# A Taylor-feature attention and a six-layer local-attention transformer in one kernel: first transfers, block sums, Wo's product and the order list changed

## Chip, cores and metric

The kernel runs on one core of one Trainium2 chip. The metric is the device time of one launch in microseconds (us). A profiled execution gives the trace; other executions give the times.

## What is computed

Input x is 8 sequences of 512 tokens with 128 features, all float32. With `ln` a normalisation over the features without weights:

```
y = x + ln(first(ln(x)))           # first: linear attention with Taylor features
out = y + ln(stack(ln(y)))         # stack: six layers

first: q, k = h Wq', h Wk'  (16 heads of 16);  v = h Wv'  (16 heads of 64)
       f(z) = [1, z/2, (z x z)/(4 sqrt 2)];  A = tril(f(q) f(k)')
       y = A v; y = y * rsqrt(mean(y^2) + 1e-5) * g;  return y Wo'
stack, six times:
       q, k, v = split(x Wqkv); q, k = scaled unit vectors, rotary tables
       local attention over windows of 32 (own window and the one before)
       x = x + attention Wo
       x = x + (a * gelu(gate)) W2 + b2,  a, gate = split(norm(x) W1 + b1)
```

Both halves work on tokens shifted by one in half of the features. f(q)f(k)' is (1 + s/4)^2/2 + 1/2 up to a common factor, s being the product of q and k: so the kernel forms the squares, adds 1 and masks only in the 128x128 blocks on the diagonal. For the blocks left of it the "+1" is a constant times the sum of v over earlier blocks of 128 tokens. These are the block sums of the title: sums of h over the first 128, 256 and 384 tokens (`CS`, four columns, the first zero), times Wv.

## The kernel before, in words

One Python function, `order` (with the class `Order`), writes a list of stages. Every stage has a place on a time axis (`PLACE`), the list is sorted by place, and each of the five engine programs walks the list and emits its share of every stage. So the places set the order of instructions on each engine and nothing else; waits on semaphores do the rest. Each engine works in its own order and never overtakes. `group` and `put(..., banks=...)` give each stage that writes PSUM the next bank of a ring (two banks in the first attention, three in the stack) and record which stage must have freed it.

**The start.** `sync_program` issues all first transfers on SP's queue: the constants C (2756 columns), VEC, two staged constants, Wq and Wk and Wv of the first attention, its Wo, and then x of the first sequence (stage AL). GpSimd (POOL) copies Wq and Wk three times into a wider layout in AO (L1250), ScalarE (ACT) rounds all weights to float32r in WH, six pieces (L1001), and VectorE (DVE) takes the rest, WL = w - WH (L783), after it has cast the staged constants. Only then do ACT and DVE start on the list.

**The first attention** has 24 slots for each of 8 sequences (b): AL transposes x, N1 to N4 normalise it (N4 spreads the factor, AX multiplies it in, on DVE, and forms `CS` by three reductions, L806), AC multiplies the block sums by Wv (16 float32 products of 128x128 weights by 4 columns), ACd copies them to cumt. AQ and AV are the projections, each three float32r products (high by high, high by low, low by high), AS the scores, ASa the square (ACT), ASd the mask (DVE), AY scores by v, AE adds the block sums to AY's result. AR, AI, AM and AO finish: root mean square and Wo. All of it is software-pipelined over b by the places.

**The stack** has units u = 8 layer + b, each of 8 slots n (384 slots in all) and 4 pairs m of slots. PJ projects q and k of two heads (2 per slot), PQ squares (ACT, L1177), PT multiplies by the rotary tables (DVE, L891), TS swaps rows by DMA (SP, L445), AD adds the swapped rows (POOL, L1312), SS sums squares, NM1 and NM2 make the norms, RW and RB write them out and spread them over 64 partitions by DMA (SP, L453 and L463), PR multiplies k by them (POOL, L1294). S1 (PE) needs both PR of its pair; then MX (DVE, L915, L920), S3 (exponentials, ACT, L1201), SU (DVE, L926), NP (POOL, L1317), TT (DVE, two transposes, L936 and L937), PX (SP, DMA PP<-PX, L470), PV (PE, four parts), PVn (ACT copy to AOT, L1214). Once per unit: WO (eight float32 products AOT by LO on PE in one piece, 16 records in the trace; two adds on DVE), F1 to F3 (normalisation; F2n on DVE is L956 to L960, F3 spreads on PE, H on DVE, XCH on ACT, XCL by POOL in F3l), F4g and F4a (three pairs of products, GELU and gate), F5. XS and XSl round the next unit's input.

Every product on PE stands at L480 in the trace, since all go through the helper `mm`; float32 products leave two records each, float32r ones a single record. A row names the moving operand first and the weights second: PS<-LXH,LH is PJ's first product, PS<-LH,LXH is VP's (the v projection), PS<-CS,WH is AC's.

Of the kernel before, what the change touches and what calls it, by code (L numbers as in the profile page):

```python
# [6 lines left out]
F32 = mybir.dt.float32  # L7
# [8 lines left out]
F1 = 341  # L16
# [20 lines left out]
    "AVa": -0.03, "AS": -1.00, "ASa": -0.95, "ASd": -0.82, "AY": 0.90, "AE": 2.85, "AEa": 3.56,  # L37
    "AR": (14.32, 25.00), "AI": (25.06, 26.09, 27.44), "AM": (28.75, 0.64), "AMd": 0.10, "AO": (30.62, 0.53),
    "NM": (35.69, 37.69, 37.84, 40.22), "AZ": 39.99, "NX": (44.40, 45.04, 45.20, 47.87), "AW": 47.72,
}  # L40

CONST = {}
# [93 lines left out]
def order():  # L136
# [94 lines left out]
    for u in range(NB * DEPTH):  # L231
# [6 lines left out]
        at(z + P["WO"], group, "WO", u, "wo_dve", 2 * u + 2)  # L238
# [44 lines left out]
def build(nc, xin, cst, awq, awk, awv, awo, wqkv, wo, w1, w2, vec, out):  # L283
    o = order()
    no = o.no
    with ExitStack() as ctx:
# [13 lines left out]
        with ExitStack() as ca:  # L300
# [7 lines left out]
            CS = [sb(f"CS{i}", [128, 4], F32, ca) for i in range(2)]  # L308
            XR = [sb(f"XR{i}", [128, L], F32, ca) for i in range(4)]
# [97 lines left out]
        def sync_program(e):  # L407
            on = Waits(e)
            e.dma_start(C[:, :], cst[:, 0:KEPT]).then_inc(sem["c_in"], 16)
            e.dma_start(VEC[:, :, :], vec).then_inc(sem["vec_in"], 16)  # L410
            n_sel = CONST_COLS - KEPT
            e.dma_start(Vf[:, 0:n_sel], cst[:, KEPT:CONST_COLS]).then_inc(sem["sel_in"], 16)
            e.dma_start(Vf[:, 3072:3328], awq).then_inc(sem["awq_in"], 16)
# [3 lines left out]
            for st, key in o.line:  # L417
                if st == "AL":
                    b, = key
                    if b:  # L420
                        on.wait_ge("al_pe", b)
# [55 lines left out]
        def tensor_program(e):  # L477
# [14 lines left out]
            for st, key in o.line:  # L492
# [208 lines left out]
                elif st == "WO":  # L701
# [5 lines left out]
                    for hp in range(8):  # L707
                        p = mm(bk(st, key)[:, :], LO[:, hp, :], AOT[:, hp, :], hp == 0, hp == 7)
# [674 lines left out]
```

## Time and profile before

| | |
|---|---|
| median of three runs | 3833.57 us (3826.7 to 3837.46) |
| profiled execution | 3838.31 us, span of its records 3836.5 us |
| PE busy | 3549.6 us (93%) |
| DVE, ACT, POOL busy | 2627.8, 2549.0, 2022.4 us (68, 66, 53%) |
| chain that ended last | PE 69%, DVE 12%, ACT 7%, issue 5%, DMA 3%, SPq 2%, POOL 1% |
| first transfers | C 1378 KB, two staged constants 768 KB, Wv and Wo 512 KB each, x 256 KB, Wq and Wk 128 KB each |

A span is cut into stretches by time from its first record. Busy is the time in which an engine had an instruction in work; PE's is modelled from pipelined products, so the start-to-start distance of its rows says more than their durations. PEclk is the granted clock of TensorE as a share of 2.4 GHz: 0.50 is 1.2 GHz. "[0.88 <-X]" after a row is time in which the engine sat idle before it, and what ended that. The chain is followed back from the last instruction, each step to what released it.

### The profile page before, as it was taken

How to read it: one execution, taken by the hardware profiler on the slowest of the kernel's cores; microseconds unless marked ns; L12 is line 12 of the kernel's file. 1: busy time of each engine (PE TensorE's matmuls, PEld its weight loads, DVE VectorE, ACT ScalarE, POOL GpSimd, SP SyncE). 2: the span in 40 equal slices, each digit the busy share in tenths (PEclk: the TensorE clock that was granted, in tenths of full speed). 3: DMA queues.
4: the chain of work that ended last, by engine and by line, in shares of the span. 5: the costliest groups of instructions: out<-in, count | busy, mean ns of one | idle time of the engine just before them, and what ended most of it. 6: DMA issues, size and time to landing. Idle time of an engine off the chain costs nothing.

```text
span 3836.5 us, 149435 instructions
## 1 busy us (share of the span) xinstructions
PE 3549.6 (93%) x65224; PEld 2293.5 (60%) x65416; DVE 2627.8 (68%) x3583; ACT 2549.0 (66%) x5965; POOL 2022.4 (53%) x1564
## 2 busy tenths in 40 slices
PE   7999998799999999999999999999999999999997
PEld 4555554466666666666666666666666666666664
DVE  3555555577777777777776777777777777767662
ACT  4655564476767676777666766777767767677773
POOL 0000000666666666666666666666666666666651
PEclk9999999799999999999999999999999999999997
DMA  1000000333333333333333433333433333433330
GB/s 49 6 6 6 6 6 3 130 129 117 123 125 132 121 124 121 122 130 129 118 121 114 138 123 123 115 124 121 136 117 128 113 132 120 134 113 126 126 109 25
DMA packets 222618, 389.72 MB, mean 102 GB/s; under 512 B 63758, under 2 KB 101900, under 8 KB 221836
## 3 DMA queue, kind: packets, MB, share of 16 engines
q1 hardware_dynamic: 196080, 364.42, 27.5%
q10 hardware_dynamic: 25884, 15.73, 1.4%
q8 instruction: 514, 8.42, 0.9%
q14 instruction: 140, 1.15, 0.1%
HBM read 124.14 MB, written 7.34 MB: 34 GB/s over the span
## 4 chain that ended last, share of the span: by engine, by line
PE 69%; DVE 12%; ACT 7%; issue 5%; DMA 3%; SPq 2%; POOL 1%; ACTq 0%; POOLq 0%; DVEq 0%
PE PS L480 68%; ACT SC L1201 4%; DVE MX L915 2%; DMA RB<-root_scratch 2%; DVE TPB L891 2%; DVE SM L926 2%; DVE PX L937 1%; DMA PP<-PX 1%; POOL K L1294 1%; DVE VAR L958 1%; ACT AOT L1214 1%; DVE H L965 1%; ACT XCH L1072 1%; DVE VAR L956 1%; DVE BQ L920 1%
## 5 line engine op out<-in xcount | busy, mean ns | idle before, releaser
L891 DVE SCALAR_TENSOR_TENSOR TPB<-PS,VEC,C 128x1024 f32<-128x1024 f32 x768 | 961.0, 1263 | 98.4 <-ACT SX L1177 89.2
L1201 ACT ACTIVATE SC<-PS,BQ,RQ 128x64 f32<-128x64 f32 x3072 | 966.2, 430 | 26.0 <-DVE BQ L920 25.6
L1294 POOL TENSOR_TENSOR K<-K,RB 128x512 f32<-128x512 f32 x384 | 492.4, 1282 | 727.2 <-DMA RB<-root_scratch 726.7
L480 PEld LDWEIGHTS PS<-PP,VV 32*64 32x64 f32 x24576 | 436.1, 133 | 314.0 <-issue 210.8
L480 PE MATMUL PS<-PP,VV 32*64 32x64 f32 (+1 forms) x24576 | 542.0, 223 | 72.1 <-ACT AOT L1214 32.9
L1177 ACT ACTIVATE SX<-PS 128x512 f32<-128x512 f32 x768 | 475.5, 628 | 195.0 <-PE PS L480 188.8
L926 DVE TENSOR_REDUCE SM<-SC 128x16 f32<-128x1024 f32 x192 | 234.2, 1220 | 388.7 <-ACT SC L1201 388.6
L1312 POOL TENSOR_TENSOR K<-TPB,TR 128x512 f32<-128x512 f32 x384 | 493.8, 1286 | 0.0
L1312 POOL TENSOR_TENSOR Q<-TPB,TR 128x512 f32<-128x512 f32 x384 | 492.9, 1284 | 0.0
L1317 POOL TENSOR_TENSOR SC<-SC,RC 128x1024 f32<-128x1024 f32 x192 | 366.2, 1907 | 158.1 <-DVE RC L928 154.5
L480 PE MATMUL PS<-LXH,LH 128*128 128x512 f32 x768 | 350.2, 456 | 16.9 <-DVE TPB L891 9.8
L1191 ACT COPY VV<-PS 128x512 f32<-128x512 f32 x384 | 238.3, 620 | 188.6 <-PE PS L480 185.5
L1214 ACT COPY AOT<-PS 128x1024 f32<-128x1024 f32 x192 | 197.3, 1028 | 248.0 <-PE PS L480 246.1
L480 PE MATMUL PS<-AOT,LO 128*128 128x512 f32 x768 | 338.6, 594 | 0.0
L480 PEld LDWEIGHTS PS<-K,Q 64*32 64x32 f32 x24576 | 255.8, 105 | 126.2 <-issue 80.5
L480 PE MATMUL PS<-K,Q 64*32 64x64 f32 (+1 forms) x24576 | 294.1, 225 | 35.0 <-issue 19.4
L480 PE MATMUL PS<-LXH,LL 128*128 128x512 f32 x768 | 305.4, 398 | 0.0
L480 PE MATMUL PS<-LXL,LH 128*128 128x512 f32 x768 | 304.9, 397 | 0.0
L1260 POOL TENSOR_TENSOR XR<-XR,T 128x512 f32<-128x512 f32 x8 | 12.9, 1611 | 524.0 <-DVE T L862 524.0
L480 PE MATMUL PS<-SX,C 128*32 128x128 f32 x6144 | 253.3, 281 | 4.8 <-ACT SX L1177 3.0
L1133 ACT ACTIVATE PA<-PS 128x768 f32<-128x768 f32 (+1 forms) x192 | 169.8, 884 | 128.2 <-PE PS L480 127.1
L915 DVE TENSOR_REDUCE MX<-PS 128x16 f32<-128x1024 f32 x192 | 234.0, 1219 | 25.4 <-PE PS L480 24.7
(166 smaller groups left out, 6076.8 us busy)
## 6 DMA issues: line engine op xcount, KB each, us to landing
TR<-TPB SPq DMA_DIRECT2D x768, 256.0 KB, 2.7
RB<-root_scratch SPq DMA_DIRECT2D x768, 128.0 KB
PP<-PX SPq DMA_DIRECT2D x192, 192.0 KB, 2.6
WS<-in_wqkv ACTq DMA_DIRECT2D x72, 128.0 KB, 2.5
PP<-PX SPq DMA_DIRECT2D x192, 48.0 KB, 2.3
root_scratch<-NV SPq DMA_DIRECT2D x384, 8.0 KB
LO<-in_wo ACTq DMA_DIRECT2D x6, 512.0 KB, 4.6
T<-in_x SPq DMA_DIRECT2D x8, 256.0 KB, 3.0
```

The lines of the kernel that those rows point to most:

```text
L480: return e.matmul(dst, lhsT, rhs, start=start, stop=stop, **kw)
L891: e.scalar_tensor_tensor(TPB[:, n % 3:4 + n % 2:3 + n % 2 - n % 3, w, :], g, VEC[:, l, 9 + w:10 + w], C[:, at:at + 1024].rearrange("p (o c ...
L915: e.tensor_reduce(MX[:, :], g, AX_X, ALU.max).then_inc(sem["s1_dve"], 1)
L926: e.tensor_reduce(SM[:, :], SC[m % 2][:, :, :, :].rearrange("p g x k -> p g (x k)"), AX_X, ALU.add).then_inc(sem["su_dve"], 1)
L1133: e.activation(P[t % 3][:, :, 0:n], PS[:, 2 * (t % 2):2 * (t % 2) + 2, 0:n], ACT.Square, bias=1.0, scale=0.25).then_inc(sem["as_act"], 1)
L1177: e.activation(SX[i % 3][:, :], bk("PJ", key)[:, :], ACT.Square).then_inc(sem["pj_act"], 1)
L1191: e.copy(VV[:, c, 512 * hf:512 * hf + 512], bk("VP", key)[:, :]).then_inc(sem["vp_act"], 1)
L1201: p = e.activation(SC[m % 2][:, g, :, :].rearrange("p x k -> p (x k)"), bank[s][:, at:at + 64], ACT.Exp, bias=BQ[m % 2][:, g:g + 1], scale ...
L1214: e.copy(AOT[:, 2 * p % 8:2 * p % 8 + 2, :], PS[:, 2:4, :]).then_inc(sem["pv_act"], 1)
L1294: e.tensor_tensor(dst, dst, RB[n % 2][:, :], ALU.mult).then_inc(sem["pr_pool"], 1)
L1312: e.tensor_tensor((Q, K)[w][:, n % 8, :], TPB[:, n % 3, w, :], TR[n % 2][:, w, :], ALU.add).then_inc(sem["ad_pool"], 1)
L1317: e.tensor_tensor(sc, sc, RC[m % 2][:, :].rearrange("p (g o) -> p g o", o=1).broadcast_to([128, 16, 64]), ALU.mult).then_inc(sem["np_pool" ...
```

## The change

C is loaded in two transfers: columns 0 to 707 first, the rotary tables (2048 columns) last with a semaphore of their own (`tab_in`), for which the first PT waits. x of sequence 0 is SP's second transfer. Wq, Wk and Wv of the first attention are issued on ACT's queue, ahead of its table load. DVE splits `CS` into a float32r high part and the rest (`CX`, eight columns, two more small instructions for each b), and AC takes 16 float32r products, of 8 and of 4 columns, in place of 16 float32 ones; ACd adds the two halves by a reduction. WO's product becomes a stage WO (the first two of eight products) and three stages WOp (two each), each with its own wait for PVn; the adds on DVE follow the last. All places are new.

Sorted, the new places change the order of the stack as follows. The unit that the rows show is that of slots 192 to 199 (pairs m = 96 to 99, PJ 400 to 415), in the trace from 1985 to 2048 us.

- PE: the third part of PV stands ahead of the two SS of its slot, was behind. WO(23) stood between PJ(409) and the fourth part of PV(96); its pieces now stand ahead of PJ(409): WO, PV(96, 2), SS, SS, WOp, WOp, WOp, PJ(409). F3 stood ahead of PJ(413), now behind.
- Banks: VP, PJ, WO, F1 to F5 and RQ take three banks in turn. PJ(410) took its bank from PJ(409) and takes it from WO; F1 took it from WO and takes it from PJ(409); PJ(414) took it from F3 and takes it from PJ(413), which is free once PT(413) has run on DVE.
- DVE: TT stands ahead of NM1, was behind; WO's adds stand ahead of PT(409), were behind.
- POOL: the two AD of a slot stand ahead of its PR, were behind; XSl stands behind the next PR, was ahead.
- ACT: XS stands ahead of VC. SP: the order is the same.

In the first attention AS stands some 0.4 slots earlier, AE 0.3 earlier, AV ahead of N1 for the first sequences; AC stays behind AR and between two AS.

```diff
@@ -26,17 +26,18 @@
 PLACE = {
-    "S1": 0.07, "MX": 0.18, "S3": (0.52, 0.62, 1.38, 1.44), "SU": 1.45, "NP": 1.74, "TT": 2.63, "PX": 2.78,
-    "PV": (3.60, 3.67, 4.87, 5.14), "PVn": 5.23, "PJ": (-7.60, -7.06), "PQ": (-7.54, -7.13),
-    "PT": (-7.37, -6.95), "TS": -6.56, "SS": -6.40, "AD": -5.68, "NM1": -3.39, "NM2": -2.98, "RW": -2.86,
-    "RQ": -1.78, "RB": -2.15, "PR": -1.83, "XS": -9.54, "XSl": -9.24, "VP": -0.60, "VC": -0.55, "WO": 13.08,
-    "F1": 13.91, "F2": 14.08, "F2n": 14.42, "F3": 14.93, "F3l": 14.71, "TB": (15.66, 15.92),
-    "F4": (15.76, 15.79, 15.83), "F5": 17.32, "E1": 18.17, "EN": (18.53, 19.02, 19.08, 19.73), "E2": 19.50,
-    "E3": 20.36, "AL": -35.20, "NI": (-33.38, -31.57, -31.13, -29.38), "AX": -29.38, "AXp": -29.48,
-    "AC": -22.55, "ACd": -22.70, "AQ": (-8.65, -8.07), "AQa": 0.01, "AQd": 0.03, "AV": (-9.18, 2.33),
-    "AVa": -0.03, "AS": -1.00, "ASa": -0.95, "ASd": -0.82, "AY": 0.90, "AE": 2.85, "AEa": 3.56,
-    "AR": (14.32, 25.00), "AI": (25.06, 26.09, 27.44), "AM": (28.75, 0.64), "AMd": 0.10, "AO": (30.62, 0.53),
-    "NM": (35.69, 37.69, 37.84, 40.22), "AZ": 39.99, "NX": (44.40, 45.04, 45.20, 47.87), "AW": 47.72,
+    "S1": 0.070, "MX": 0.204, "S3": (0.520, 0.817, 1.345, 1.440), "SU": 1.481, "NP": 2.090, "TT": 2.494,
+    "PX": 2.428, "PV": (3.608, 3.721, 4.542, 5.121), "PVn": 5.291, "PJ": (-7.527, -7.038),
+    "PQ": (-7.490, -7.100), "PT": (-7.376, -6.920), "TS": -6.667, "SS": -6.381, "AD": -5.837, "NM1": -3.382,
+    "NM2": -3.273, "RW": -2.978, "RQ": -1.794, "RB": -2.203, "PR": -1.824, "XS": -9.729, "XSl": -8.095,
+    "VP": -0.654, "VC": -0.535, "WO": (12.494, 12.664, 12.743, 12.755), "F1": 13.903, "F2": 14.160,
+    "F2n": 14.420, "F3": 15.011, "F3l": 15.140, "TB": (15.648, 16.315), "F4": (15.746, 15.781, 15.832),
+    "F5": 17.288, "E1": 17.542, "EN": (18.253, 18.621, 18.733, 19.195), "E2": 19.234, "E3": 20.274,
+    "AL": -33.742, "NI": (-32.832, -32.109, -30.652, -29.154), "AX": -29.060, "AXp": -26.947, "AC": -22.855,
+    "ACd": -22.643, "AQ": (-8.619, -8.246), "AQa": -0.094, "AQd": -0.306, "AV": (-9.421, 2.424), "AVa": -0.196,
+    "AS": -1.374, "ASa": -1.037, "ASd": -0.890, "AY": 0.975, "AE": 2.559, "AEa": 3.552, "AR": (15.747, 25.047),
+    "AI": (25.064, 25.483, 27.445), "AM": (28.750, 0.727), "AMd": -0.720, "AO": (30.708, 0.580),
+    "NM": (35.565, 37.690, 38.161, 40.725), "AZ": 40.998, "NX": (44.350, 45.008, 45.145, 46.999), "AW": 46.923,
 }
@@ -235,7 +236,9 @@
             at(z + j + P["VC"], o.put, "VC", 8 * u + j)
-        at(z + P["WO"], group, "WO", u, "wo_dve", 2 * u + 2)
+        at(z + P["WO"][0], group, "WO", u, "wo_dve", 2 * u + 2)
+        for i in range(1, 4):
+            at(z + P["WO"][i], o.put, "WOp", u, i)
         at(z + P["F1"], group, "F1", u, "f1_act", 2 * u + 2)
@@ -306,6 +309,7 @@
             CS = [sb(f"CS{i}", [128, 4], F32, ca) for i in range(2)]
+            CX = [sb(f"CX{i}", [128, 8], F32R, ca) for i in range(2)]
             XR = [sb(f"XR{i}", [128, L], F32, ca) for i in range(4)]
@@ -406,19 +410,19 @@
             on = Waits(e)
-            e.dma_start(C[:, :], cst[:, 0:KEPT]).then_inc(sem["c_in"], 16)
-            e.dma_start(VEC[:, :, :], vec).then_inc(sem["vec_in"], 16)
+            tab = CONST["tab"][0]
+            e.dma_start(C[:, 0:tab], cst[:, 0:tab]).then_inc(sem["c_in"], 16)
+            e.dma_start(T[2][:, :].rearrange("p (a d) -> p a d", a=4),
+                        xin[0].rearrange("(a p) d -> p a d", p=128)).then_inc(sem["x_in"], 16)
             n_sel = CONST_COLS - KEPT
             e.dma_start(Vf[:, 0:n_sel], cst[:, KEPT:CONST_COLS]).then_inc(sem["sel_in"], 16)
-            e.dma_start(Vf[:, 3072:3328], awq).then_inc(sem["awq_in"], 16)
-            e.dma_start(Vf[:, 3328:3584], awk).then_inc(sem["awk_in"], 16)
-            e.dma_start(AOf[:, 2048:3072], awv).then_inc(sem["awv_in"], 16)
             e.dma_start(WOA[:, :, :], awo.rearrange("p (c d) -> p c d", c=8)).then_inc(sem["awo_in"], 16)
+            e.dma_start(VEC[:, :, :], vec).then_inc(sem["vec_in"], 16)
+            e.dma_start(C[:, tab:KEPT], cst[:, tab:KEPT]).then_inc(sem["tab_in"], 16)
             for st, key in o.line:
-                if st == "AL":
-                    b, = key
-                    if b:
-                        on.wait_ge("al_pe", b)
+                if st == "AL" and key[0]:
+                    b, = key
+                    on.wait_ge("al_pe", b)
                     e.dma_start(T[2][:, :].rearrange("p (a d) -> p a d", a=4),
@@ -546,16 +550,15 @@
                     b, = key
-                    on.wait_ge("cs_dve", 3 * b + 3)
+                    on.wait_ge("cs_dve", 5 * b + 5)
                     on.wait_ge("aw_act", 6)
                     on.wait_ge("aw_dve", 6)
-                    on.wait_ge("zero_pool", 2)
                     free(on, st, key)
...
                         c = slice(2048 + 128 * hp, 2176 + 128 * hp)
-                        mm(g[:, 4 * hp:4 * hp + 4], WH[:, c].bitcast(F32), CS[b % 2][:, :], hp == 0, False, skip_group_check=True)
-                        p = mm(g[:, 4 * hp:4 * hp + 4], WL[:, c].bitcast(F32), CS[b % 2][:, :], False, hp == 7, skip_group_check=True)
+                        mm(g[:, 8 * hp:8 * hp + 8], WH[:, c], CX[b % 2][:, :], hp == 0, False, skip_group_check=True)
+                        p = mm(g[:, 8 * hp:8 * hp + 4], WL[:, c], CX[b % 2][:, 0:4], False, hp == 7, skip_group_check=True)
                     p.then_inc(sem["ac_pe"], 1)
@@ -703,10 +706,16 @@
                     free(on, st, key)
-                    on.wait_ge("pv_act", 4 * u + 4)
-                    for hp in range(8):
-                        p = mm(bk(st, key)[:, :], LO[:, hp, :], AOT[:, hp, :], hp == 0, hp == 7)
-                    p.then_inc(sem["wo_pe"], 1)
+                    on.wait_ge("pv_act", 4 * u + 1)
+                    for hp in range(2):
+                        mm(bk(st, key)[:, :], LO[:, hp, :], AOT[:, hp, :], hp == 0, False)
+                elif st == "WOp":
+                    u, i = key
+                    on.wait_ge("pv_act", 4 * u + i + 1)
+                    for hp in range(2 * i, 2 * i + 2):
+                        p = mm(bk("WO", (u,))[:, :], LO[:, hp, :], AOT[:, hp, :], False, hp == 7)
+                    if i == 3:
+                        p.then_inc(sem["wo_pe"], 1)
                 elif st == "F1":
@@ -804,6 +813,12 @@
                         e.tensor_reduce(CS[b % 2][:, i:i + 1], T[3][:, 0:128 * i], AX_X, ALU.add).then_inc(sem["cs_dve"], 1)
+                    on.wait_ge("zero_pool", 2)
+                    on.wait_ge("cs_dve", 5 * b + 3)
+                    e.tensor_copy(CX[b % 2][:, 0:4], CS[b % 2][:, :]).then_inc(sem["cs_dve"], 1)
+                    on.wait_ge("cs_dve", 5 * b + 4)
+                    e.tensor_tensor(CX[b % 2][:, 4:8], CS[b % 2][:, :], CX[b % 2][:, 0:4].bitcast(F32),
+                                    ALU.subtract).then_inc(sem["cs_dve"], 1)
                 elif st == "AQd":
@@ -818,7 +833,8 @@
                         on.wait_ge("ae_dve", 8 * (b - 1))
-                    e.tensor_copy(cumt[b % 2][:, :], bk("AC", key)[:, 0:32]).then_inc(sem["ac_dve"], 1)
+                    g = bk("AC", key)[:, 0:64].rearrange("p (h x i) -> p h i x", h=8, x=2)
+                    e.tensor_reduce(cumt[b % 2][:, :].rearrange("p (h i) -> p h i", h=8), g, AX_X, ALU.add).then_inc(sem["ac_dve"], 1)
                 elif st == "ASd":
@@ -882,6 +898,7 @@
                     at = CONST["tab"][0] + 1024 * w
+                    on.wait_ge("tab_in", 16)
                     if n > 1:
@@ -935,10 +952,10 @@
                     e.transpose(PX[:, :, :], SC[m % 2][:, :, 0, :]).then_inc(sem["tt_dve"], 1)
-                elif st == "WO":
-                    u, = key
+                elif st == "WOp" and key[1] == 3:
+                    u = key[0]
                     l, b = lb(u)
-                    g = bk(st, key)
+                    g = bk("WO", (u,))
                     x0, x1 = X[0:64, b, 0:L], X[64:128, b, 1:1 + L]
@@ -990,6 +1007,9 @@
 
+            e.dma_start(Vf[:, 3072:3328], awq).then_inc(sem["awq_in"], 16)
+            e.dma_start(Vf[:, 3328:3584], awk).then_inc(sem["awk_in"], 16)
+            e.dma_start(AOf[:, 2048:3072], awv).then_inc(sem["awv_in"], 16)
             table("natural_log_exp_and_others")
@@ -1088,7 +1108,7 @@
                         on.wait_ge("ax_pool", b)
-                        on.wait_ge("cs_dve", 3 * b)
+                        on.wait_ge("cs_dve", 5 * b)
                     elif kind == "mid" and b:
```

## Rows read from the trace of the kernel before

**Rows 1.** Busy time by stretch (us): PE, weight loads, DVE, ACT, POOL; PEclk, DMA, GB/s

```profile
50.00:640.00 590.00, 584.98 (x2940) 301.51 (x2938) 325.65 (x592) 347.79 (x552) 19.32 (x13) 0.97 0.02 6
...
760.00:3740.00 2980.00, 2781.42 (x60386) 1873.69 (x60580) 2198.21 (x2829) 2104.22 (x5200) 1929.19 (x1480) 1.00 0.36 123
```

**Rows 2.** First transfers: stretch 3 to 12; Wq's to landing; chain's last step

```profile
3.00:12.00 9.00, 0.00 (x0) 0.00 (x0) 2.07 (x4) 1.15 (x3) 2.35 (x6) 1.00 0.98 386
...
VA<-in_awq SPq DMA_DIRECT2D x1, 128.0 KB, 7.3
...
4.66 8.28 DMA T<-in_x
```

**Rows 3.** Timeline, 9 to 32 us: start, duration, engine, line, operation, idle before

```profile
9.50 2.35 POOL L1250 COPY AO<-VA 128x256 f32<-128x256 f32 x6 [6.88 <-DMA VA<-in_awq]
10.85 3.22 ACT L1001 CAST WH<-AO 128x512 fp32r<-128x512 f32 x6 [8.84 <-POOL AO L1250]
11.50 3.90 DVE L783 TENSOR_TENSOR WL<-AO,WH 128x512 fp32r<-128x512 f32 x6 [0.95 <-ACT WH L1001]
14.20 0.59 ACT L1079 COPY XR<-PS 128x512 f32<-128x512 f32 x1
19.50 0.16 DVE L794 TENSOR_SCALAR N<-PS 128x4 f32<-128x4 f32 x1 [4.11 <-PE PS L480]
24.82 0.59 PE L480 MATMUL PS<-CS,WH 128*128 128x4 f32 x2 [1.96 <-DVE CS L806]
31.25 0.57 PE L480 MATMUL PS<-CS,WL 128*128 128x4 f32 x2
```

**Rows 4.** AC: busy time on PE, 40 to 600; timeline of AC(4) and AC(6)

```profile
40.00:600.00 560.00, 31.09 (x224) 0.97 0.02 6
...
276.55 0.39 PE L480 MATMUL PS<-CS,WH 128*128 128x4 f32 x2
...
280.22 1.09 PE L480 MATMUL PS<-PA,VA 128*64 128x384 f32 x4
...
434.31 0.56 PE L480 MATMUL PS<-CS,WH 128*128 128x4 f32 x2
```

**Rows 5.** PE by stretch: behind AC(1), between, behind AC(7)

```profile
52.00:64.00 12.00, 12.00 (x63) 0.72 0.00 0
64.00:116.00 52.00, 51.85 (x274) 1.00 0.02 6
...
516.00:520.00 4.00, 4.00 (x15) 0.57 0.00 0
```

**Rows 6.** Timeline of PE: short float32r products, and what follows them

```profile
102.90 0.45 PE L480 MATMUL PS<-QA,KA 64*128 64x256 f32 x4
103.28 0.87 PE L480 MATMUL PS<-PA,VA 128*64 128x384 f32 x4
```

**Rows 7.** Whom PE waited for, 760 to 3740: total us, times, longest

```profile
PE PS L480 <- DVE TPB L891: 60.1, 53, 1.2
...
PE PS L480 <- DMA PP<-PX: 26.7, 37, 1.8
PE PS L480 <- DVE VAR L960: 19.9, 44, 1.2
PE PS L480 <- POOL K L1294: 11.5, 20, 1.2
```

**Rows 8.** Timeline of the unit of slots 192 to 199, by engine

```profile
1999.84 1.66 SPq L445 DMA_DIRECT2D TR<-TPB  x2
...
2008.45 1.28 POOL L1294 TENSOR_TENSOR K<-K,RB 128x512 f32<-128x512 f32 x1 [3.64 <-DMA RB<-root_scratch]
...
2015.65 7.03 PE L480 MATMUL PS<-AOT,LO 128*128 128x512 f32 x16
...
2037.21 1.27 DVE L891 SCALAR_TENSOR_TENSOR TPB<-PS,VEC,C 128x1024 f32<-128x1024 f32 x1
...
2037.56 0.40 PE L480 MATMUL PS<-LXH,LH 128*128 128x512 f32 x1
```

## The prediction

> **What bounds the kernel now.** First the busy time by stretch [rows 1]. It shows three parts. From 50 to 640 us, in the first attention, PE is busy for 585.0 of 590 us: only PE's own work can shorten it, new places at most the 5.0 us of idle time. From 760 to 3740 us, in the stack, PE is idle for 199 us of 2980, some 4.3 us in each of 46 units, with DVE at 74% and ACT at 71%: here the order counts, and so does the question which wait ends last. Between and after them lie ramps. Second the granted clock: 0.97 in the first attention, 1.00 in the stack [rows 1]. Third the timeline of the start, where the span begins with 13 us in which PE waits for x [rows 2].
>
> **The start.** The last step of the chain is x, landed at 12.94 us behind all constants and weights [rows 2]. The DMA engines are full: 386 GB/s from 3 to 12 us at a share of 0.98. The queue carries 3730 KB up to and with x, 3.82 MB; 3.82 / 0.386 = 9.9 us, so a landing is at 3.0 us plus the megabytes ahead / 0.386. Test on Wq: 2322 KB give 9.2, measured 2.1 + 7.3 = 9.4 [rows 2]. After the change Wq and Wk (256 KB, and as much beside them on the other queue) land at 4.4, x (354 + 256 KB, as much beside) at 6.2, Wv at 7.1, the staged constants (2.20 MB) at 8.7, where they were.
> ACT converts WH before it touches the list. From POOL's start at 9.50 WH began 1.35 us later and took 3.22 [rows 3]: from 4.4 that ends at 9.0, in place of 14.1. XR moves from 14.20 to 9.0: 5.2 us. DVE begins no earlier, but it waited 0.95 us for WH [rows 3]; without this WL ends at 14.3, and DVE's next task, at 19.50 before, is due at 14.3: just covered. If not, the chain is late by what WL is late. AC(0) then starts at 24.82 - 5.2 + 0.4 (two small DVE instructions of 0.16 us and their gaps, the price of the row at 19.50 [rows 3]) = 20.0. It lasted to 31.25 + 0.43 = 31.68 [rows 3], 6.85 us for 32 records, and 16 records of the same distance take 3.4: it ends at 23.4, 8.3 us earlier. Bounds: 4 us, if the queues share otherwise and the first conversions come late, and 10 us.
>
> **AC of the other seven sequences.** AC lies in the stretch where PE has no slack, so its time counts in full. Seven AC keep PE busy for 31.09 us (224 records); AC(4), at the full clock throughout, takes 280.22 - 276.55 = 3.67 us, 0.115 for a record [rows 4]. A float32r product is one record. The trace has none of 4 or 8 columns; the nearest are four with 128 to 256 columns and 64 rows, which take 103.28 - 102.90 = 0.38 us, at most 0.095 each with its weights [rows 6]. I take the 0.115 of a float32 record, since it is as wide in weights: 7 x 16 x 0.115 = 12.8 us, gain 18.3. Bounds: a product costs as much as a whole float32 one (0.23, no gain) or nearly nothing (gain 31).
> [...]
>
> **The clock behind AC.** Behind each AC the clock falls to 0.50, 1.2 GHz: 12 us at a mean of 0.72 around AC(1) and 4 us at 0.57 behind AC(7), with 1.00 between [rows 5]. Four of the seven cost 12 x 0.28 = 3.4 us, three 4 x 0.43 = 1.7: 18.7 us in all, which is what 0.97 over 590 us says. Of this 31.09 - 7 x 3.67 = 5.4 lie inside AC and are counted above, 13.3 in the work behind it. A fall can begin early: in AC(6) the ninth of 16 pairs of records, at 434.31, is the first slow one (0.56 us), 8 x 0.23 = 1.8 us after AC's start [rows 4]. Nothing else in this part sets one off [rows 5]. An AC of 1.8 us is at the edge. I expect one of seven to remain, 1.7 us: gain 11.6. Bounds: all stay at 1.7 (gain 13.3 - 11.9 = 1.4), none (13.3).
> DVE's two added instructions and the reduction in ACd cost nothing while DVE is busy for 55%. AC's neighbours stay. The new places of AS, AE and AQ can win the 5.0 us of idle time [rows 1]; I take 2, bounds -3 and 5.
>
> **The stack.** I expect nothing, though PE waits there. The longest wait is F4's second pair for a bank: 60.1 us in 53 waits, 1.2 us at most, so nearly once in each unit, on TPB, that is PT(414) [rows 7]. PT(414) stands behind SU(99) on DVE, that behind S3(99) and XCH on ACT, that behind H, F2n and MX(99): this chain runs from S1(99)'s end, and the change moves none of its members against another. What PE gains inside it is waited out at its end. F3 behind PJ(413) removes the wait on VAR (19.9 us, 0.45 each [rows 7]): hidden.
> In return PJ(414) now waits for PT(413). That ran from 2037.21 to 2038.48 while PE began PJ(414) at 2037.56 [rows 8]: a new wait of 0.9 us, under the 1.2 us of the F4 wait. Without that cover it costs 48 x 0.9 = 43 us.
> WO is 7.03 us in 16 records [rows 8], the same in four pieces; what it passes, PJ(409), is delayed by 7 us, and behind it PQ, PT(409) and the swap by DMA for AD(408, 409). PV's last part, for which ACT waits, keeps its time, and DVE and POOL are idle during WO. PJ(410)'s bank now comes from WO's two adds, free 0.5 us before by my count of the durations.
> SS behind WO's first piece (7.03 / 4 = 1.8 us) delays NM1, which TT no longer waits for: these two about cancel, off the chain.
> POOL is the delicate place. PR(197) feeds S1(98). It waited 3.64 us for RB until 2008.45; now two AD of 1.28 us stand ahead of it. They need the swapped rows, issued from 1999.84 to 2001.5 and landed some 2.7 us later (the page's median), 4.2 us before PR: enough for 2.6 us of AD, with 1.6 to spare [rows 8]. Where the landings lie closer, PR is late by up to 2.6 us. Sum of the stack 0, bounds -12 and +12 us for the small shifts.
>
> **Sum.** 8.3 + 18.3 + 11.6 + 2 = 40.2. Against the profiled execution, 3838.31: 3798. That lies 4.7 us over the median of the runs, 3833.57, so the time is 3793. Its own range, with the start at 4 to 10 and the stack's bounds, is 3781 to 3807.
>
> **Rivals.**
> Clock falls stay behind all seven AC: for it speaks the fall that began 1.8 us after AC's start; 10.2 us less gain: 3803. Chance 0.12.
> The float32r products are no cheaper than float32 ones: 18.3 and 11.6 go, and 3.4 of the start: 3826, no change. Rows 6 speak against it. Chance 0.05.
> The weights load faster than any row shows: 7 x 16 x 0.085 = 9.5 us more and the last fall gone, 3782. Rows 6 allow it no more than they ask for it. [...] Chance 0.06.
> The stack's gaps close: the waits on PX, VAR and K together are 58.1 us [rows 7], TT ahead of NM1 and AD in POOL's idle time would shorten them, and half of it gives 3764. Against it: they lie inside chains that end in later waits. Chance 0.14.
> Slower: AD ahead of PR makes S1 late. PE waits for PR already 20 times, 11.5 us [rows 7]. If the swapped rows land less than 2.6 us before RB, each S1 of that kind starts later; at 2.6 us once a unit it is 48 x 2.6 = 125 us, at a typical 1.4 it is 67: 3860. It decides from 52 / 48 = 1.1 us a unit on. Chance 0.08.
> The forecast has 0.55.
>
> **How the numbers follow.** A measurement here tells 0.3% (11.5 us) from no change. Faster than 3822 are the forecast, the first, third and fourth rival: 0.87, less a little for mixtures: 0.86. Within 0.3%: 0.07. Slower: 0.07. The range for 8 in 10 goes from 3766, with part of the closing gaps, to 3821, where small losses in the stack meet falls that stay.
>
> **What would show it.** XR at 9 us, AC(0) from 20 to 23.5. AC(4) at 1.8 us from its first record to the next product's. A clock of 0.99 or more over the first attention, with at most two falls. In the stack the same 65 us a unit, the VAR wait gone, a new wait of PJ(414) on TPB and a smaller one of F4; PR no later than 1.3 us behind the landing of RB. Wrong it is if the clock still falls behind most AC, if AC takes over 2.5 us, or if the period of a unit moves by more than 0.3 us.

## The result, and the profile after

The kernel after took 3814.36 us in the median of 8 runs (3809.55 to 3820.37) beside 3834.79 for the kernel before: a ratio of 0.9947 with a 95% interval of 0.9934 to 0.9961, 20 us faster. A second comparison gave 0.9938 [0.9924, 0.9951]. The forecast was 3793, 41 us faster. The profiled execution of after took 3809.55, 4.8 us under its median, while that of before, 3838.31, lay 3.5 over its own: the pair of traces shows 28.8 us, the medians show 20.4.

Three views of the kernel after follow: busy time by stretch (columns of [rows 1]), the same narrowed to the products with CX, which are AC's, from 40 to 600 us, and PE by stretch; the releasing lines are numbered some 20 higher than before:

```profile
50.00:640.00 590.00, 573.36 (x2877) 285.69 (x2878) 339.37 (x625) 349.94 (x561) 18.69 (x14) 0.98 0.02 6
...
760.00:3740.00 2980.00, 2791.28 (x60293) 1870.38 (x60292) 2247.37 (x2816) 2101.31 (x5180) 1913.88 (x1463) 1.00 0.36 122
```
```profile
40.00:600.00 560.00, 13.63 (x112) 0.99 0.02 6
```
```profile
52.00:64.00 12.00, 12.00 (x59) 1.00 0.00 1
...
104.00:116.00 12.00, 12.00 (x63) 0.86 0.00 1
...
328.00:344.00 16.00, 16.00 (x82) 0.89 0.00 1
...
480.00:492.00 12.00, 12.00 (x63) 0.86 0.00 1
```

AC of seven sequences takes 13.63 us in 112 records, where [rows 4] had 31.09 in 224. The clock falls to its lower level behind three of the seven, by 1.7, 1.8 and 1.7 us (12 x 0.14, 16 x 0.11, 12 x 0.14), and no longer behind AC(1), which [rows 5] showed.

The start (timeline, columns of [rows 3]):

```profile
10.00 3.69 DVE L792 TENSOR_TENSOR WL<-AO,WH 128x512 fp32r<-128x512 f32 x6
10.23 0.58 ACT L1099 COPY XR<-PS 128x512 f32<-128x512 f32 x1
...
20.41 1.26 POOL L1276 TENSOR_TENSOR XL<-T,XH 128x512 fp32r<-128x512 f32 x1 [13.14 <-ACT XH L1131]
20.89 0.81 DVE L818 CAST CX<-CS 128x4 fp32r<-128x4 f32 x1
21.73 0.17 DVE L820 TENSOR_TENSOR CX<-CS,CX 128x4 fp32r<-128x4 f32 x1
21.95 0.29 PEld L484 LDWEIGHTS PS<-CX,WH 128*128 128x128 f32 x1 [3.37 <-DVE CX L820]
```

AC(0) ran from 21.95 to 25.39 (its last product begins at 25.17, and they are 0.22 us apart), where it ran from 24.82 to 31.68: 6.3 us earlier at its end.

The stack can be measured by ACT's exponentials, from the first to the last (one row per kernel, before and then after; durations are min/median/max in ns, the two times are the first and the last start):

```profile
L1201 ACT ACTIVATE SC<-PS,BQ,RQ x3072: 387/421/525, 732.2 to 3765.9; 128x64 f32<-128x64 f32 x192
```
```profile
L1221 ACT ACTIVATE SC<-PS,BQ,RQ x3072: 386/422/526, 696.3 to 3737.6; 128x64 f32<-128x64 f32 x192
```

All that lies ahead of the stack gives 35.9 us in this pair of traces; a second trace of the same kernel has its first exponential at 699.2, which would be 33.0. The stack itself grew from 3033.7 to 3041.3. That is not yet the price of its new order: two traces of the order of before with the same start (the first experiment) have 3020.3. PE's waits in the stack (760 to 3710 us), where [rows 7] had 60.1 us in 53 waits on TPB:

```profile
PE PS L484 <- DVE TPB L908: 119.0, 159, 1.1
...
PE PS L484 <- DMA PP<-PX: 18.4, 26, 1.8
PE PS L484 <- POOL K L1314: 9.8, 21, 0.9
...
PE PS L484 <- DVE VAR L977: 0.4, 2, 0.2
```

Added up by place over the 46 units of this stretch, the waits on TPB are four in place of one. F4's wait, 1.24 us on average in 44 units before, is 1.06 in 46. PJ(414)'s, which was forecast, is 0.81 us in 46 units, 37.4 us in all. The product of VP ahead of it waits 0.49 us in 44 units, 21.5 us, which was not forecast. The fourth stands behind F5: 23 of the 46 units have it, and it is 11.0 us in all. Here it is in its place (timeline of after):

```profile
2019.80 1.27 DVE L908 SCALAR_TENSOR_TENSOR TPB<-PS,VEC,C 128x1024 f32<-128x1024 f32 x1
...
2020.99 0.28 DVE L921 TENSOR_TENSOR NV<-NV 128x128 f32<-128x128 f32 x1
2021.12 1.27 POOL L1332 TENSOR_TENSOR Q<-TPB,TR 128x512 f32<-128x512 f32 x1 [4.39 <-DVE TPB L908]
2021.31 1.24 DVE L923 SCALAR_TENSOR_TENSOR NV<-NV 128x128 f32<-128x128 f32 x1
...
2022.37 1.31 POOL L1332 TENSOR_TENSOR K<-TPB,TR 128x512 f32<-128x512 f32 x1
2022.58 1.24 DVE L925 SCALAR_TENSOR_TENSOR NV<-NV 128x128 f32<-128x128 f32 x1
...
2023.75 1.27 DVE L908 SCALAR_TENSOR_TENSOR TPB<-PS,VEC,C 128x1024 f32<-128x1024 f32 x1
...
2025.07 0.49 PE L484 MATMUL PS<-LXH,LH 128*128 128x512 f32 x1 [0.63 <-DVE TPB L908]
```

NM2's operations at L923 and L925 take 0.29 us where no GpSimd instruction runs. Here each lasts until 0.15 us behind the end of the GpSimd addition that ran when it began (2021.12 + 1.27 = 2022.39, and it ends at 2022.55). It is so throughout the stack: 124 of NM2's operations take over 0.6 us in the trace of after, 59 in that of before, and all of them end 0.14 to 0.16 us behind the end of a GpSimd instruction. PT behind them is 1.9 us late (two operations of 1.24 us in place of 0.29), and PE's projection waits 0.63 us for the bank. These two additions, AD(414, 415), now stand ahead of PR, in time in which GpSimd had waited for the root.

### The profile page after: what moved, and what is told of

It reads as the page before. It is cut to its first block, busy times and chain, and to the rows that moved or that the text cites. A ratio compares the mean times of both kernels' runs of the same rounds, so it can differ in the third digit from the quotient of the medians.

```text
span 3807.8 us, 149416 instructions
## 1 busy us (share of the span) xinstructions
PE 3533.7 (93%) x65288; PEld 2266.8 (60%) x65288; DVE 2700.3 (71%) x3599; ACT 2553.1 (67%) x5965; POOL 2025.9 (53%) x1564
## 4 chain that ended last, share of the span: by engine, by line
PE 65%; DVE 16%; ACT 7%; issue 5%; DMA 3%; SPq 2%; POOL 2%; ACTq 0%; POOLq 0%; DVEq 0%
PE PS L484 64%; ACT SC L1221 4%; DVE TPB L908 4%; DVE MX L932 3%; DMA RB<-root_scratch 2%; DVE SM L943 2%; ACT AOT L1234 1%; DVE PX L954 1%; DVE VAR L973 1%; POOL K L1314 1%; DVE H L982 1%; DVE PP L953 1%; DVE NV L923 1%; ACT XCH L1092 1%; DMA PP<-PX 1%
## 5 line engine op out<-in xcount | busy, mean ns | idle before, releaser
L1221 ACT ACTIVATE SC<-PS,BQ,RQ 128x64 f32<-128x64 f32 x3072 | 966.1, 430 | 29.2 <-DVE BQ L937 28.4
L484 PE MATMUL PS<-LXH,LH 128*128 128x512 f32 x768 | 370.9, 483 | 62.9 <-DVE TPB L908 56.0
L484 PE MATMUL PS<-AOT,LO 128*128 128x512 f32 x768 | 351.2, 600 | 0.0
L484 PEld LDWEIGHTS PS<-LXH,LH 128*128 128x128 f32 x768 | 145.0, 189 | 184.3 <-DVE TPB L908 89.2
L484 PEld LDWEIGHTS PS<-AOT,LO 128*128 128x128 f32 x768 | 141.8, 190 | 152.8 <-issue 148.5
```

The costliest lines, as they stand in the source:

```text
L484: return e.matmul(dst, lhsT, rhs, start=start, stop=stop, **kw)
L1221: p = e.activation(SC[m % 2][:, g, :, :].rearrange("p x k -> p (x k)"), bank[s][:, at:at + 64], ACT.Exp, bias=BQ[m % 2][:, g:g + 1], scale ...
```

## Experiments

"Without the stack part" names the kernel with the start, the float32r sums and the attention's new places, and the stack's order of before. Edits are against before or after, as said. Each ratio is to the kernel before on the same chip.

### First: which part gives, which takes

**Without the stack part** (after, edited; the second run is a repeat):

```
-    "S1": 0.070, "MX": 0.204, ... "WO": (12.494, 12.664, 12.743, 12.755), ...
+    "S1": 0.07, "MX": 0.18, ... "WO": 13.08, ...      # all names of the stack as before
```

> The change without its stack part: the transfers of the start, the float32r sums and the new places of the first attention; every place of the stack, and Wo's product in one piece, as before. Theory 1 (the first attention gives all that the profiles show, 36 us, and the new order of the stack takes back 8 to 16): 36 us faster than before, 3798 to 3801, and the whole stack keeps 3028 us from its first scores to its last. Theory 2 (the stack is neutral; the pair of profiles shows its 8 us by accident, and the first attention gives less in the median): 20 us faster, 3814, as the whole change.

> The kernel without the stack part once more, beside the others of this call. If the stack part costs what the first comparison said: 0.990, and 15 us faster than the whole change stood in its two comparisons (0.9947 and 0.9938). If that was one chip's: 0.992 to 0.994.

Measured 3791.78 us, ratio 0.9902 [0.9889, 0.9914], and again 3791.66, 0.9911 [0.9898, 0.9923]. The stack part costs 10 to 17 us, by the four ratios: (0.9938 or 0.9947) - (0.9902 or 0.9911), 0.0027 to 0.0045 of 3830; the interval of each ratio adds some 5 us either way. Theory 1 holds, with the stack at 3020.3 us in both traces where it said 3028. Without the stack part the gain is 34 to 38 us, where the forecast's sum, which had the stack at nothing, was 40.2. (The ratios count here: on this chip the kernel before took 3831.25 and 3825.13 us.)

**The stack part alone** (before, edited):

```
-    "S1": 0.07, "MX": 0.18, ... "WO": 13.08, ...
+    "S1": 0.070, "MX": 0.204, ... "WO": (12.494, 12.664, 12.743, 12.755), ...
```

> The kernel before, with nothing of the change but the places of the stack and Wo's product in four pieces. Theory 1: 8 to 16 us slower than before (3843 to 3851), with PE's waits on the two DVE copies out of the rotation going from 60 to about 119 us. Theory 2: no change, within 3 us of 3835.

Ratio 1.0015 [1.0005, 1.0024], 6 us slower, and 109.8 us of waits on TPB (760 to 3710 us). The waits are those of theory 1, the loss is a little under its lower end; theory 2, within 3 us of no change, still touches the interval of 2 to 9 us, so this kernel alone does not rule it out.

**Float32r sums alone, start alone, both** (before, edited; the two hunks of the diff as they stand):

```
+            CX = [sb(f"CX{i}", [128, 8], F32R, ca) for i in range(2)]
...
+            e.dma_start(Vf[:, 3072:3328], awq).then_inc(sem["awq_in"], 16)
```

> The kernel before with the float32r sums alone (split on DVE, products of 8 and 4 columns, reduction in the copy); start, places and Wo as before. My sum: 18.3 in seven AC, 3.4 in the first, 10 in the clock behind: 32 us by the prediction; by what the traces show since (three falls instead of one stay) 28: 3807. Rival, the new places of the attention do a part of it: under 22 us, above 3813, with falls behind most AC as before.

> The kernel before with the new order of the first transfers alone. Prediction: x's copy at 9.0 in place of 14.2, 5 us faster, 3830. Rival: DVE's weight split, which needs the same weights, ends no earlier and DVE is then the late one: 2 us or less, 3833.

> The start's transfers and the float32r sums together, with all places of before in the first attention as in the stack. By the traces the two give 25 + 3 us up to the stack's first scores, and the new places of the attention 4 more: 0.9925 (29 us faster). Rival, from the medians (21 + 3 for the two alone, 38 with the places): 0.9937, so that the attention's places are worth 12 to 14 us.

Ratios 0.9945 [0.9931, 0.9959], 0.9992 [0.9983, 1.0001] and 0.9935 [0.9923, 0.9946]: 21, 3 and 25 us. The first is under the 28 expected and just inside the rival's 22, but not by the rival's mechanism: in its trace, too, the clock falls behind three AC. The second lies between its two expectations and is not clear of no change; the third is at its rival's 0.9937. In the traces the stack's first exponential comes 25.3, 3.3 and 29.2 us earlier than before. With the attention's places it comes 32.1 and 32.8 us earlier: these are worth 3 to 4 us there, while the ratios say 9 to 13 (0.9935 against 0.9911 and 0.9902), with intervals of 5 us each way. How much of that is theirs stays open.

### Second: taking one piece out of the new order

The whole change again, and with Wo in its old place, F3 in its old place, GpSimd's four steps in theirs:

```
-    "WO": (12.494, 12.664, 12.743, 12.755),
+    "WO": (13.08, 13.08, 13.08, 13.08),
```
```
-    "F3": 15.011, "F3l": 15.140,
+    "F3": 14.93, "F3l": 14.71,
```
```
-    "AD": -5.837, "PR": -1.824, "NP": 2.090, "XSl": -8.095,
+    "AD": -5.68, "PR": -1.83, "NP": 1.74, "XSl": -9.24,
```

> The whole change again, beside the three kernels that undo one part of its stack order. The kernel without the stack part stood at a ratio of 0.9902, so the stack part takes back 17 us there. Expected here: 0.9947 again, 20 us faster than before. Rival: the difference between the two was one of chips, and the whole change gains 30 us or more here.

> The whole change, with Wo's product in one place again (behind the second projection of the slot, its four pieces without a gap). Theory W (Wo ahead of that projection costs: PE stands before its first piece's neighbours, the projection's two DVE copies and what waits for their banks come 7 us late): 10 us or more faster than the whole change, and the waits on the copies out of the rotation go from 119 to under 80 us. Theories F (F3's place) and G (GpSimd's additions) expect no change, within 4 us of the whole change.

> The whole change, with F3 ahead of PJ(413) again and its place on the other engines. Theory F (F3 behind PJ(413) makes PJ(414) take the bank that PT(413) frees last, and every later product of the rotation with it): 10 us or more faster than the whole change; the waits on TPB fall by 40 us and those on VAR come back with 19. Theories W and G: within 4 us of the whole change.

> The whole change, with GpSimd's additions AD behind PR again, as well as NP and the low part of X where they were. Theory G (AD now fall on the root's small DVE operations between SBUF tiles, 0.29 us becomes 1.24 us each, and PT behind them is late for PE): 8 us or more faster than the whole change, NV's operations back at 0.29 us, BQ's median back from 338 to 268 ns. Theories W and F: within 4 us of the whole change.

Ratios: whole 0.9938 [0.9924, 0.9951], Wo back 1.0052 [1.0039, 1.0065], F3 back 0.9947 [0.9934, 0.9961], GpSimd back 1.0018 [1.0009, 1.0028]. All three theories fall in this form: none of the undone pieces makes it faster, two make it 44 and 31 us slower. With GpSimd back NM2's operations are at 0.29 us again (L923: median 292 ns), as theory G said, and the kernel is slower all the same. With F3 back the waits are close to those of before (62.6 us on TPB, 21.4 on VAR, 30.5 on AOT; before 58.8, 19.9 and 32.6 in the same stretch) and the time is that of the whole change: F3's move trades waits and is worth nothing, as the prediction had it.

The trace of Wo back has a new wait on TPB in one place, behind Wo, 1.31 us in each of 46 units, 60.4 us in all (timeline):

```profile
2000.82 0.68 DVE L961 TENSOR_TENSOR X<-PS,X 64x512 f32<-64x512 f32 x1 [3.61 <-PE PS L484]
2001.54 0.69 DVE L962 TENSOR_TENSOR X<-PS,X 64x512 f32<-64x512 f32 x1
...
2002.26 1.28 DVE L908 SCALAR_TENSOR_TENSOR TPB<-PS,VEC,C 128x1024 f32<-128x1024 f32 x1
...
2003.60 0.50 PE L484 MATMUL PS<-LXH,LH 128*128 128x512 f32 x1 [1.31 <-DVE TPB L908]
```

DVE stands idle for 3.61 us at Wo's adds, with PT(409) behind them in its queue. The new place of PT(409), 20 - 6.92 = 13.08, ties with Wo's old 13.08, and the tie falls to Wo. The kernel before had 13.05: PT first.

### Third: adding one piece, and Wo in one piece

The first is after with Wo undivided at the place of its first piece. The other three start from the kernel without the stack part and put in Wo's new places, GpSimd's four steps, and the rest but F3.

```
-    "WO": (12.494, 12.664, 12.743, 12.755),
+    "WO": (12.494, 12.494, 12.494, 12.494),
```

> The whole change, with Wo's four pieces in one place, that of the first piece (12.494), ahead of the attention's last product and SS. Theory P (the breaks between the pieces cost: in the trace of the whole change the records of Wo are 10 us longer in 38 units, and those of the projection behind them 12 to 18 us): 10 us faster than the whole change (0.9915), Wo's records back at 592 ns. Theory S (what counts is that SS comes ahead of most of Wo, for the root behind it): 10 us or more slower than the whole change (0.9965 or more).

> The kernel without the stack part (ratio 0.9902), with Wo's product at its new place and in pieces alone; GpSimd and all else as before. Theory E (each part of the new order costs by itself, together 17 us): between 0.9902 and 0.9947, 10 us slower than the kernel without the stack part, as Wo's records get longer. Theory J (the parts are tied: Wo's place needs GpSimd's new order, whose undoing cost 30 us): 20 us or more slower than it (0.9955 or more).

> The kernel without the stack part (ratio 0.9902), with GpSimd's new order alone (AD ahead of PR, NP and X's low part later). Theory E: 5 us slower than it, by NV's and BQ's operations on DVE. Theory J: GpSimd's order is harmless without Wo's new place, within 4 us. My rival of the prediction, AD making PR late for S1: 20 us or more slower, with the waits on POOL K above 20 us.

> The kernel without the stack part (ratio 0.9902), with all new places of the stack but those of Wo, of GpSimd's four steps and of F3: the attention's third part ahead of SS, TT ahead of NM1, X's high part behind RQ, the small shifts. Theory E: within 5 us of it, these moves pass nothing long. Theory J, by what undoing Wo's place alone cost (46 us, the projection's copies late for their banks): here too PE waits longer for TPB, 15 us or more slower (0.994 or more).

Ratios 1.0273 [1.0259, 1.0287], 0.9989 [0.9979, 0.9999], 0.9966 [0.9953, 0.9978], 1.0028 [1.0017, 1.0039]. That is Wo undivided, then Wo, GpSimd and the rest added. For Wo and for the rest the size is that of theory J; its mechanism, parts that are tied to each other, isn't shown by it, and for the rest the fourth group finds another. GpSimd's order costs 21 to 25 us alone. That was the number of my rival, but not by its mechanism: PE waits 10.8 us for POOL K, as before. It waits for TPB at the projection behind F5, 16.0 us in 32 units, where the kernel without the stack part has no such wait. What did change on DVE are NM2's operations. The rows of NV (min/median/max in ns), for before, for GpSimd's order added, and for after:

```profile
L904 DVE TENSOR_TENSOR NV<-NV x96: 271/278/1440, 711.9 to 3720.9; 128x128 f32<-128x128 f32 x96
L906 DVE SCALAR_TENSOR_TENSOR NV<-NV x96: 291/292/1244, 712.2 to 3721.2; 128x128 f32<-128x128 f32 x96
```
```profile
L912 DVE TENSOR_TENSOR NV<-NV x96: 270/760/1402, 679.1 to 3698.6; 128x128 f32<-128x128 f32 x96
L914 DVE SCALAR_TENSOR_TENSOR NV<-NV x96: 291/1239/1251, 679.4 to 3699.0; 128x128 f32<-128x128 f32 x96
```
```profile
L921 DVE TENSOR_TENSOR NV<-NV x96: 271/906/1384, 676.0 to 3694.9; 128x128 f32<-128x128 f32 x96
L923 DVE SCALAR_TENSOR_TENSOR NV<-NV x96: 291/1236/1255, 676.3 to 3695.2; 128x128 f32<-128x128 f32 x96
```

Wo undivided is 128 us slower than the whole change (125 by the other ratio). It is the order of DVE's tasks at its worst: the adds come with the last piece, so at 12.494 they stand ahead of TT, NM1 and PT(408).

```profile
2034.47 0.68 DVE L961 TENSOR_TENSOR X<-PS,X 64x512 f32<-64x512 f32 x1 [6.52 <-PE PS L484]
...
2037.45 1.27 DVE L908 SCALAR_TENSOR_TENSOR TPB<-PS,VEC,C 128x1024 f32<-128x1024 f32 x1
...
2038.78 0.50 PE L484 MATMUL PS<-LH,LXH 128*128 128x512 f32 x1 [1.64 <-DVE TPB L908]
```

PE waits 1.64 us here in each of 46 units, 75.3 us, and behind it for AOT in 28 of them, 16.8 us: 92 us of the 128, and the rest was not followed. Theory P falls. The number of theory S holds, but it named the wrong follower (SS, which PE issues), where it is DVE's queue.

### Fourth: the two causes by themselves

**One pair of AD behind PR again** (after, edited), and in it Wo in one piece, with its adds behind NM2:

```
-            at(n + P["AD"], o.put, "AD", i)
+            at(n + (-5.68 if n % 8 == 7 else P["AD"]), o.put, "AD", i)
```
```
+    "WO": (12.74, 12.74, 12.74, 12.74),
```

> The whole change, with one pair of GpSimd's additions in each unit of eight slots (AD(414, 415) and its like, slot 8u + 7) behind PR again; everything else as in the whole change. Theory C (collision): in the whole change these two additions run beside NM2's three operations on DVE, which take 1.25, 1.24 and 0.29 us instead of three times 0.29; the PT behind them comes 1.9 us late, and the projection behind F5 waits 0.65 us for its bank. Without it that wait goes: 48 x 0.65 = 31 us, less what later waits take back; 15 to 30 us faster than the whole change, a ratio of 0.986 to 0.990, and NM2's operations there at 0.29 us. Rival W (the wait is taken back at the next one, for the transposed rows by DMA, as I argued for F4's wait): within 5 us of the whole change, 0.993.

> The kernel with one pair of AD put back (0.9906), and in it Wo's product in one piece at 12.74: on PE behind SS and ahead of PJ(409), on DVE its two adds behind NM2. What the pieces are worth by themselves. Theory P1 (the first piece, ahead of the attention's product and SS, only delays SS and NM1, off the chain): within 3 us of that kernel, 0.990 to 0.991. Theory P2 (the piece covers the wait for the transposed rows): 5 us slower, 0.992.

Measured 3787.55 us, 0.9906 [0.9892, 0.9919], and 3789.54, 0.9910 [0.9896, 0.9924]. The same place in the first of them, and its NV rows:

```profile
2074.49 0.28 DVE L921 TENSOR_TENSOR NV<-NV 128x128 f32<-128x128 f32 x1
...
2074.81 0.29 DVE L923 SCALAR_TENSOR_TENSOR NV<-NV 128x128 f32<-128x128 f32 x1
2075.13 0.29 DVE L925 SCALAR_TENSOR_TENSOR NV<-NV 128x128 f32<-128x128 f32 x1
...
2075.87 1.28 DVE L908 SCALAR_TENSOR_TENSOR TPB<-PS,VEC,C 128x1024 f32<-128x1024 f32 x1 [0.45 <-ACT SX L1197]
...
2077.78 0.40 PE L484 MATMUL PS<-LXH,LH 128*128 128x512 f32 x1
```
```profile
L923 DVE SCALAR_TENSOR_TENSOR NV<-NV x96: 291/292/1245, 678.3 to 3668.6; 128x128 f32<-128x128 f32 x96
```

The wait of 0.63 us is gone, and with it 12 to 16 us of time (0.9938 and 0.9947 against 0.9906). Within the intervals that is all that the stack part had cost: this kernel stands beside the one without the stack part. Theory C holds, with its size at the lower end or just under. The 31 us that it started from, 48 x 0.65, took the unit of the timeline for every unit. The trace of after has that wait in 23 of 46 units, 11.0 us in all, the second trace of the same kernel has 8.4 in 16 units, and this one none. The wait that went is about the time that came back. Why the other units were spared wasn't followed, and the edit moves the pair on GpSimd as a whole, so that what it may have changed beside the collision is not told apart. P1 holds: Wo's pieces are worth nothing measurable.

**PT(409) ahead of Wo's adds** in the two slow kernels (Wo back, and the rest of the places added):

```
-    "WO": 13.08
+    "WO": 13.10
```

> The whole change, with Wo's product in one place behind PJ(409), at 13.10 instead of 13.08, so that on DVE its two adds come behind PT(409) as they did before the change. With 13.08 (46 us slower than the whole change) they stood ahead of PT(409), waited 3.6 us for Wo's end, and PE waited 1.3 us a unit for PT(409) right behind: 48 x 1.3 = 62 us. If that is the whole of it, this kernel is 46 us or more faster than that one: 0.993 or less. If Wo's place itself counts (it starts 7 us later against SS and the root), it stays above 0.998.

> The kernel that added the rest of the new places to the one without the stack part (1.0028, 46 us slower than it), with Wo at 13.10 instead of 13.08, so that PT(409) stands ahead of Wo's two adds on DVE again. If the order of these two DVE tasks is what cost the 46 us, as in the other kernel of this kind (1.0052 to 0.9951): 0.992 to 0.9935. If the other new places cost by themselves: above 0.998.

The ratios are 0.9951 [0.9934, 0.9967] in place of 1.0052, and 0.9912 [0.9897, 0.9927] in place of 1.0028: 39 and 44 us back for two hundredths of a slot, which change the order of two DVE tasks. The 46 us expected in the first came out as 39, the time itself 2 thousandths over the bound. The remaining places, without GpSimd's, Wo's and F3's, are worth nothing either way. Four kernels end at 0.9902 to 0.9912, all faster than the change as made, and not to be told apart: the stack's order of before is as good as any of the new ones.

Not followed to the end are Wo's pieces alone (0.9989; its trace has 44.2 us of waits on TPB ahead of F1, in 45 units, the whole change none) and GpSimd's order undone in the whole change (1.0018; its waits on VAR are 33.5 us).

## Why the prediction went wrong

The step that failed is a term of the sum, "Sum of the stack 0, bounds -12 and +12 us". Measured it is +10 to +17 us, and the cause is two additions on GpSimd that lengthen NM2 on DVE.

- Its reasoning on PE's own chain held in its result. F3's move traded waits at no gain; PJ(414) waits 0.81 us a unit where 0.9 was forecast; the VAR wait went (0.4 us left); WO in pieces costs nothing; PR is not late for S1 (POOL K 9.8 us). The cover was another than forecast. F4's wait shrank only from 1.24 to 1.06 us. Against PJ(414)'s 37.4 us and VP's 21.5 stand mainly the waits on VAR (19.9 to 0.4 us) and on AOT (32.6 to 4.1).
- What it left out is the step "POOL is the delicate place". I asked whether the two AD ahead of PR end in time for PR, and they do. I didn't ask what runs on DVE in the time in which GpSimd had been idle. That was NM2 and, behind it, a PT for which PE waits. With one pair of AD a unit back behind PR the loss is gone (0.9906). The slower rival had the right two instructions and the wrong victim.
- The row that would have told it was in the trace of before: GpSimd waits 3.64 us for RB [rows 8], and NV's operations in the same trace show 271/278/1440 ns, four to five times their median in some cases. Here that spread, in an operation of fixed shape, is a wait that the view books as duration.
- The Trainium skill states the rule, in "SBUF — State Buffer", section "Who interferes with whom": a DVE instruction with two SBUF inputs contends with a GpSimd instruction that reads SBUF, and the port pair that they share is an exclusive lock. The traces agree: NM2's operations take 0.29 us alone and 1.24 beside AD, while TPB's copy, with one of its two inputs from PSUM, takes the same beside a GpSimd instruction as without one (1.22 to 1.29 us, and 1.24 to 1.29).

The other terms, each with its measured size:

- Start: 8.3 forecast, 6.3 measured. XR came at 10.23 in place of 9.0: Wv landed at 9.19 where 7.1 was forecast, and ACT's last two roundings waited for it. Another 0.65 us of AC(0)'s lateness is the cast of CX, 0.81 us beside the split of X on GpSimd, where I had priced it at 0.16. That looks like the same exclusion, since the cast ends within 0.03 us of the GpSimd instruction; but all eight casts run beside one (810/890/900 ns), so no run shows the cast alone.
- AC: 18.3 forecast, 31.09 - 13.63 = 17.5 measured. A float32r product costs 13.63 / 112 = 0.12 us with the falls in it; AC(4) takes 1.88 us, from 256.72 to 258.60, 0.117 a product, where 1.8 was forecast. The rival in which the weights load faster took 0.085 us off each product. No run shows such a term, and it falls. By the Trainium skill, "TensorE: Matmul & The Clock Gate", section "Weight-path perf modes", fast weight load is on for 128 weights of an input type that isn't FP32. No faster load shows here in float32r.
- Clock: 11.6 forecast. Three falls, which cost 5.2 us together, stay instead of one of 1.7: 13.3 - 5.2 = 8.1.
- Places of the attention: 2 forecast; what remains in the traces is 35.9 - 6.3 - 17.5 - 8.1 = 4.0.

Up to the stack that is 35.9 in place of 40.2, 4 us short (2 to 6 by the ratios without the stack part), and the stack is 10 to 17 over: together about the 21 that were missed (3814 against 3793). The sign of being wrong, "if the period of a unit moves by more than 0.3 us", had too wide a bound: 0.3 x 48 = 14 us is the whole loss.

## What to carry to other kernels

When a task moves into an engine's idle time, list what the other engines run in that time and whether it takes longer beside the task. Here GpSimd's additions made small DVE operations between SBUF tiles four times as long. And count a wait over all units before multiplying: the one of the timeline stood in half of them. A task that waits long (here Wo's adds) belongs behind everything in its queue that others wait for; in the two kernels in which a tie of two numbers had put them ahead of PT(409), that order was worth 39 and 44 us, more than the 10 to 17 that the whole new order of the stack costs. Single pieces taken out of an order planned as one measure the break, not the piece: repair the tie first, then compare.

## What the runs showed of the hardware

The exclusion between the engines ends with GpSimd's instruction. A 128x128 operation between SBUF tiles took 1.24 us beside an addition of 1.27 us and 0.27 to 0.29 alone, and the long ones ended 0.14 to 0.16 us behind a GpSimd instruction. A cast of four columns took 0.81 to 0.90 us beside one, and no run has it alone. TPB's copy, with one input from PSUM, was untouched: 1.22 to 1.29 us. The transposes of 128x512 from SBUF were untouched too: 0.66 to 0.67 us (PX) with and without a GpSimd instruction beside them.

Float32r products of 4 and 8 columns with 128x128 weights took 0.117 us each (1.88 us for 16), as long as a record of a float32 product of 4 columns (0.115). Behind an AC of 16 such products the clock fell to its lower level, 1.2 GHz, in three of seven cases, and behind an AC of 32 float32 records in all seven (the kernel before).
